# Softmax of the last attention block: half of its exponents taken head by head, with the maximum as bias and sums kept by ScalarE

## The chip, the cores and the metric

The kernel runs on one core of a Trainium2 chip. The core has five engines that run their own instruction queues in order and meet at semaphores: TensorE (PE, with weight loads shown as PEld), VectorE (DVE), ScalarE (ACT), GpSimd (POOL) and SyncE (SP, which issues the DMAs here). The metric is the device time of one execution in microseconds. The kernel before takes 341.5 us, the median of 3 runs that lie between 341.49 and 341.51.

## The reference

The inputs are `x` and `ctx_1024`, both 32 x 64 x 128, and a score bias of 32 x 16 x 64 x 64. Two layers follow each other. The first has two attentions with 16 heads of 8 columns and a feed-forward part, each followed by a layer norm; the second is one attention with 16 heads of 64 columns, the bias added twice:

```
def _L1_xattn_ref(q, k, v, bias, graph_attn_bias, wq, ...):     # both biases are the same array
    qh, kh, vh = heads of (q @ wq + bq), (k @ wk + bk), (v @ wv + bv)
    scores = einsum('bhqd,bhkd->bhqk', qh / sqrt(dk), kh) + bias + graph_attn_bias
    weights = softmax(scores, axis=-1)
    out = einsum('bhqk,bhkd->bhqd', weights, vh) @ wo + bo + q
    return layernorm(out) * ln_g + ln_b

x = _L0_xattn_ref(x, ctx_1024, ...)       # self attention, cross attention, feed-forward, 3 layer norms
x = _L1_xattn_ref(x, ctx_1024, ctx_1024, fside, fside, ...)
```

In the first layer a row is masked where it is all zero (`mask0`), which the kernel keeps as a sign per row.

## The kernel before, in words

The 32 sequences are taken in 16 pairs; one tile is a pair, 128 rows on 128 partitions. Each tile goes through three chains of steps, called A (self attention), B (cross attention and feed-forward) and C (the second layer). Each chain works on another tile at the same time: while C is at tile 5, A and B are some tiles ahead. Scores of a tile are 128 x 1024 numbers, 16 heads of 64; they are handled in two groups of 8 heads, called group 0 and group 1 below.

Group g of C's softmax goes through these steps. `fadd` (DVE, L973) adds bias and products in the tile `Sc`; `max` (DVE, L983) takes the maximum of each head into `C_mx`; `sub` (POOL, L1077) subtracts it from 128 x 512 scores in place; `exp` (ACT, L771) takes the exponent of 128 x 512 numbers with a scale of 2 into `Pc`; `den` (DVE, L991 and L993) sums each head into `C_den` and takes the reciprocal `C_rd`; `nrm` (POOL, L1086) multiplies. Then PE transposes the weights (`pt`, L609), ACT copies them from PSUM (`pts`, L780), PE multiplies them with the values (`zt`, L622), ACT copies (`zts`, L750), and PE makes the output projection (`o`, L632), which DVE adds to the residual (`y`, L1002). The last norm (L926 to L943 on DVE, L1033 to L1053 on POOL) and a store end the tile. From tile 12 on odd tiles of C use the score tile of A (`A_S`) and A's banks.

Chain A's `m0` step (DVE, L835 and L838) takes the largest magnitude of each row for four tiles at once and turns it into the sign, 128 x 4 numbers; it runs four times. PE has steps that only keep it at work: products of a zero tile, `K.warm` near the beginning (two products each) and `L.warm` at the end (three products each, `COOL` of them, L347), which wait for the last norm of chain B.

No scheduler runs on the chip: `PLAN` is a written list of about 1,900 words such as `C.exp_1#5`, chain, step and tile. Each engine walks through it and issues the steps that it has, so the list sets the order on all five queues. The steps wait for semaphores that count: `C.s_sub` goes up by one for each `sub`, `C.s_p` for each `exp`, `C.s_den` for each sum.

Of the kernel before, what the change touches and what calls it, by code (L numbers as in the profile page):

```python
# [1109 lines left out]
A.xh#0 A.gb#0 A.e#1 C.ks_1#3 C.clo#4 B.am#0 C.v_0#0 A.max_0#1 B.cm#0 A.qk#2 A.max_1#1 C.v_1#0 C.vs_0#0 A.q0#2  # L1110
A.sub_0#1 B.tr#0 A.e0#2 B.xts#0 A.sub_1#1 A.exp_0#1 B.qkv#0 A.nz#2 A.exp_1#1 A.cnt#2 A.pt_0#1 A.v#2 B.qk#0
A.pt_1#1 A.pts_0#1 B.q0#0 C.k_0#4 A.cut#2 A.pts_1#1 A.kblk#2 C.vs_1#0 A.pv_0#1 A.pv_1#1 B.e0#0 A.zts#1
C.ks_0#4 A.z#1 C.k_1#4 A.zn#1 C.k_0#5 A.y#1 C.ks_1#4 A.st#1 A.qkv#3 C.ks_0#5 B.nz#0 C.k_1#5 A.rstd#1 C.k_0#6
A.xh#1 C.ks_1#5 A.gb#1 B.cnt#0 A.e#2 B.cut#0 B.v#0 B.kblk#0 B.am#1 K.warm#5 A.qk#3 C.k_1#6 A.max_0#2 B.cm#1
C.ks_0#6 A.q0#3 B.tr#1 A.sub_0#2 A.e0#3 B.xts#1 A.max_1#2 C.ks_1#6 B.e#0 A.nz#3 A.exp_0#2 A.sub_1#2 A.cnt#3
B.qkv#1 B.max_0#0 A.exp_1#2 A.pt_0#2 B.max_1#0 B.qk#1 A.pt_1#2 A.pts_0#2 B.sub_0#0 C.k_0#7 A.pts_1#2 B.sub_1#0
B.exp_0#0 A.pv_0#2 A.pv_1#2 B.q0#1 A.v#3 B.e0#1 A.zts#2 A.cut#3 B.exp_1#0 A.z#2 B.pt_0#0 A.kblk#3 A.zn#2
B.pt_1#0 B.pts_0#0 B.nz#1 C.k_1#7 A.y#2 B.pts_1#0 A.st#2 B.cnt#1 C.ks_0#7 B.pv_0#0 B.cut#1 B.pv_1#0 A.rstd#2
C.v_0#1 B.v#1 B.zts#0 C.ks_1#7 B.kblk#1 A.xh#2 B.z#0 C.vs_0#1 A.e#3 B.zn#0 B.y#0 B.st#0 A.qkv#4 A.max_0#3
B.rstd#0 C.v_1#1 A.max_1#3 C.v_0#2 C.vs_1#1 B.xh#0 A.sub_0#3 A.qk#4 B.gb#0 B.e#1 C.vs_0#2 A.q0#4 A.sub_1#3  # L1120
A.exp_0#3 A.gb#2 B.f1#0 C.v_1#2 B.max_0#1 B.f1s#0 A.exp_1#3 B.max_1#1 B.f2#0 A.pt_0#3 B.f2s#0 B.sub_0#1
A.pt_1#3 C.vs_1#2 B.sub_1#1 B.f3#0 B.exp_0#1 C.v_0#3 B.y3#0 B.exp_1#1 B.pt_0#1 A.pts_0#3 B.3st#0 B.pt_1#1
A.pts_1#3 B.am#2 B.3rstd#0 A.e0#4 B.pts_0#1 A.pv_0#3 B.pts_1#1 A.nz#4 A.pv_1#3 B.3xh#0 B.pv_0#1 B.cm#2 A.m0#4
B.pv_1#1 B.3gb#0 A.zts#3 A.cnt#4 B.tr#2 B.zts#1 A.z#3 A.cut#4 C.v_1#3 B.xts#2 C.vs_0#3 A.zn#3 A.kblk#4 B.z#1
C.vs_1#3 B.qkv#2 A.y#3 B.zn#1 C.bvo#0 B.qk#2 A.st#3 B.q0#2 B.y#1 A.rstd#3 B.st#1 A.v#4 B.rstd#1 B.e0#2 A.xh#3
C.obias#0 A.gb#3 A.qkv#5 B.nz#2 B.xh#1 B.cnt#2 C.x3t#0 B.cut#2 A.e#4 B.gb#1 C.x3ts#0 B.v#2 B.kblk#2 B.am#3
B.f1#1 A.qk#5 C.q_0#0 A.max_0#4 B.f1s#1 A.max_1#4 B.f2#1 C.q_1#0 A.sub_0#4 B.f2s#1 C.x3c#0 C.qs_0#0 A.sub_1#4
B.f3#1 B.e#2 B.y3#1 A.exp_0#4 A.q0#5 B.3st#1 A.exp_1#4 A.e0#5 B.max_0#2 C.qs_1#0 B.3rstd#1 A.pt_0#4 B.max_1#2
A.pt_1#4 A.pts_0#4 B.sub_0#2 C.e#0 B.cm#3 B.3xh#1 B.exp_0#2 B.sub_1#2 B.3gb#1 A.pts_1#4 B.tr#3 C.fadd_0#0
# [174 lines left out]
```

## Times and the profile before

| | us |
|---|---|
| median of the runs | 341.5 |
| the profiled execution, its own time | 341.61 |
| its span, first to last instruction | 339.8 |
| granted TensorE clock, mean over the span | 0.995 of 2.4 GHz |
| PE busy | 320.3 (94%) |
| DVE busy | 291.3 (86%) |
| POOL busy | 241.6 (71%) |
| ACT busy | 239.9 (71%) |

The profile is of one execution. Its span leaves out 1.8 us of the execution's own time. Busy time is the union of an engine's instructions, so two that overlap count once; an instruction's duration can therefore be longer than the distance from its start to the next one's. In PE's case a matmul's latency is in its duration, so short waits between matmuls do not show as idle time.

### The profile page before, as it was taken

The page shows a single profiled execution, that of the slowest core. Times are in us where ns is not written, and L with a number is a line of the kernel's source. Part 1 is how long each engine was busy: PE and PEld are TensorE (multiplying, and loading weights), DVE is VectorE, ACT ScalarE, POOL GpSimd, SP SyncE. Part 2 cuts the span into 40 slices and gives each one's busy share as a digit, 9 for nine tenths or more (in the row PEclk, how much of TensorE's full clock was granted, in tenths as well). Part 3 has the DMA queues.
Part 4 walks back from the last instruction along what each step waited for, and adds up shares of the span by engine and source line. Part 5 has one row for each costly group of instructions (what it writes and reads, how often), then busy time and mean ns, then how long its engine had stood idle before and what let it go on. Part 6 is the DMA issues. An engine that isn't in the chain of part 4 may idle for free.

```text
span 339.8 us, 13231 instructions
## 1 busy us (share of the span) xinstructions
PE 320.3 (94%) x5328; PEld 252.3 (74%) x5333; DVE 291.3 (86%) x836; ACT 239.9 (71%) x567; POOL 241.6 (71%) x376
## 2 busy tenths in 40 slices
...
GB/s 154 332 327 210 3 0 2 3 65 4 2 4 133 2 4 2 88 57 12 54 4 3 2 141 4 11 3 33 103 2 5 0 143 3 3 17 136 2 2 31
DMA packets 13180, 17.87 MB, mean 53 GB/s; under 512 B 1601, under 2 KB 10177, under 8 KB 13121
## 3 DMA queue, kind: packets, MB, share of 16 engines
...
q14 instruction: 18, 0.14, 0.1%
...
## 4 chain that ended last, share of the span: by engine, by line
PE 56%; DVE 26%; ACT 5%; issue 5%; POOL 4%; DMA 1%; SPq 1%; POOLq 0%; ACTq 0%; DVEq 0%
PE C_E L632 5%; PE C_E L577 4%; PE B_E L451 3%; PE C_E L622 3%; PE A_E L432 3%; PE B_E L432 3%; PE C_E L593 2%; DVE A_mx L889 2%; PE A_E L451 2%; DVE A_S L897 2%; PE C_E L609 2%; PE B_E L465 2%; DVE Sc L973 2%; DVE C_den L991 2%; DVE L_xh L943 2%
## 5 line engine op out<-in xcount | busy, mean ns | idle before, releaser
L1025 POOL TENSOR_TENSOR A_kblk<-A_qk,cst 128x1024 f32<-128x1024 f32 x16 | 30.3, 1897 | 25.5 <-DVE A_qk L865 25.4
L1046 POOL TENSOR_TENSOR L_xg<-L_xh,vec_sb 128x128 f32<-128x128 f32 x64 | 29.2, 456 | 15.9 <-DVE L_xh L943 13.9
L1035 POOL TENSOR_TENSOR L_rstd<-L_ve,cst 128x1 f32<-128x1 f32 x64 | 35.1, 548 | 5.0
L1077 POOL TENSOR_TENSOR Sc<-Sc,C_mx 128x512 f32<-128x512 f32 x28 | 29.1, 1046 | 9.4 <-DVE C_mx L983 9.3
L763 ACT ACTIVATE qT<-C_E,bq 128x128 f32<-128x128 f32 x112 | 31.9, 379 | 4.1 <-PE C_E L577 3.9
L1033 POOL TENSOR_TENSOR L_ve<-L_mv,cst 128x1 f32<-128x1 f32 x64 | 12.1, 189 | 29.4 <-DVE L_mv L930 28.8
L1086 POOL TENSOR_TENSOR Pc<-Pc,C_rd 128x512 f32<-128x512 f32 x28 | 29.0, 1043 | 2.8 <-DVE C_rd L993 2.5
L1025 POOL TENSOR_TENSOR B_kblk<-B_qk,cst 128x1024 f32<-128x1024 f32 x16 | 30.3, 1897 | 0.0
L577 PE MATMUL C_E<-x3T,wq_sb 128*128 128x128 f32 x224 | 29.6, 279 | 0.4 <-ACT x3T L755 0.4
L577 PEld LDWEIGHTS C_E<-x3T,wq_sb 128*128 128x128 f32 x224 | 27.0, 192 | 1.1 <-ACT x3T L755 0.7
L632 PE MATMUL C_E<-wo_sb,C_zT 128*128 128x128 f32 x224 | 27.5, 276 | 0.1
L632 PEld LDWEIGHTS C_E<-wo_sb,C_zT 128*128 128x128 f32 x224 | 26.1, 192 | 0.7 <-ACT C_zT L750 0.6
L664 ACT ACTIVATE B_S<-B_S 128x512 f32<-128x512 f32 x32 | 19.8, 634 | 3.7 <-DVE B_S L897 3.5
L889 DVE TENSOR_REDUCE A_mx<-A_E 128x8 f32<-128x512 f32 x32 | 21.0, 680 | 1.6 <-PE A_E L439 1.5
L897 DVE TENSOR_TENSOR A_S<-A_E,A_mx 128x512 f32<-128x512 f32 x32 | 21.4, 683 | 0.3
L670 ACT COPY A_PT<-A_E 128x512 f32<-128x512 f32 x32 | 18.2, 592 | 4.1 <-PE A_E L451 3.7
L897 DVE TENSOR_TENSOR B_S<-B_E,B_mx 128x512 f32<-128x512 f32 x32 | 21.0, 679 | 0.0
L889 DVE TENSOR_REDUCE B_mx<-B_E 128x8 f32<-128x512 f32 x32 | 20.9, 679 | 0.0
L664 ACT ACTIVATE A_S<-A_S 128x512 f32<-128x512 f32 x32 | 20.1, 640 | 1.0 <-DVE A_S L897 1.0
L991 DVE TENSOR_REDUCE C_den<-Pc 128x8 f32<-128x512 f32 x28 | 18.7, 667 | 1.5 <-ACT Pc L771 1.5
L750 ACT COPY C_zT<-C_E 128x512 f32<-128x512 f32 x28 | 15.5, 590 | 6.1 <-PE C_E L622 5.9
L973 DVE TENSOR_TENSOR Sc<-f,C_E 128x512 f32<-128x512 f32 x28 | 18.4, 679 | 0.9 <-PE C_E L593 0.9
...
## 6 DMA issues: line engine op xcount, KB each, us to landing
...
```

The lines of the kernel that those rows point to most:

```text
L577: last = mm(place(n).E[g][:, j * P:(j + 1) * P], wq_sb[:, c:c + P], place(n).x3T[:], start=True, stop=True)
L632: last = mm(place(n).E[0][:, 0:D], place(n).zT[:, j].rearrange("p b c -> p (b c)"), wo_sb[:, j], start=(j == 0), stop=(j == J - 1))
L664: act.activation(v, v, ACT.Exp, scale=float(DK0) ** -0.5).then_inc(a.s_p, 1)
L763: last = act.activation(place(n).qT[:, 4 * g + j], place(n).E[g][:, j * P:(j + 1) * P], ACT.Identity, bias=bq8[:, 4 * g + j:4 * g + j + 1] ...
L889: dve.tensor_reduce(m, heads((a.E, a.X)[hf][:, :]), AX.X, ALU.max).then_inc(a.s_max, 1)
L897: tt(heads(a.S[:, hf * HALF:(hf + 1) * HALF]), heads((a.E, a.X)[hf][:, :]), m.unsqueeze(2).to_broadcast([P, 8, S]), ALU.subtract).then_inc ...
L991: dve.tensor_reduce(d, heads(place(n).P[:, g * HALF:(g + 1) * HALF]), AX.X, ALU.add).then_inc(C.s_den, 1)
L1025: tt(a.kblk[:], a.qk[:, 1].unsqueeze(1).to_broadcast([P, 8, P]), at["rmask"].unsqueeze(2).to_broadcast([P, 8, P]), ALU.mult).then_inc(a.s_ ...
L1035: tt(l.rstd[:], l.ve[:], at["power"], ALU.pow).then_inc(l.s_rstd, 1)
L1046: tt(l.xg[:], l.xh[:], l.g, ALU.mult).then_inc(l.s_xg, 1)
L1077: tt(v, v, place(n).mx[:, 8 * g:8 * g + 8].unsqueeze(2).to_broadcast([P, 8, S]), ALU.subtract).then_inc(C.s_sub, 1)
L1086: tt(pr, pr, place(n).rd[:, 8 * g:8 * g + 8].unsqueeze(2).to_broadcast([P, 8, S]), ALU.mult).then_inc(C.s_nrm, 1)
```

## The change

Group 0 is as before. For group 1 POOL no longer subtracts: it multiplies the 128 x 8 maxima by -2 (a new constant column, `twice`), and ACT takes the exponent in eight instructions of 128 x 64, one for each head, each with that head's column as bias and with the sum of its results written to `C_den`. DVE's sum of group 1 goes away, its reciprocal stays. The sign of `m0` is made by comparing with a tile of zeros in place of a comparison with a constant. There are nine `L.warm` steps in place of six. `PLAN` is a new list: the same steps and three more, in another order throughout.

```diff
-COOL = 6
+COOL = 9
-CONST = dict(ident=P, hmask=H, rmask=H // 2, bsel=2, trow=1, own=2, power=1, eps0=1, eps1=1)
+CONST = dict(ident=P, hmask=H, rmask=H // 2, bsel=2, trow=1, own=2, power=1, eps0=1, eps1=1, twice=1)
...
+        "twice": np.full((P, 1), -2.0),
...
             def c_exp(g):
                 def step(n):
-                    act.wait_ge(C.s_sub, 2 * n + 1 + g)
-                    act.activation(place(n).P[:, g * HALF:(g + 1) * HALF], place(n).S[:, g * HALF:(g + 1) * HALF],
-                                   ACT.Exp, scale=2.0).then_inc(C.s_p, 1)
+                    o = place(n)
+                    if g == 0:
+                        act.wait_ge(C.s_sub, 2 * n + 1)
+                        act.activation(o.P[:, 0:HALF], o.S[:, 0:HALF], ACT.Exp, scale=2.0).then_inc(C.s_p, 1)
+                    else:
+                        act.wait_ge(C.s_sub, 2 * n + 2)
+                        for h in range(8, 16):
+                            last = act.activation(o.P[:, h * S:(h + 1) * S], o.S[:, h * S:(h + 1) * S], ACT.Exp, scale=2.0,
+                                                  bias=o.mx[:, h:h + 1], accum_out=o.den[:, h:h + 1])
+                        last.then_inc(C.s_p, 1)
...
-                ts(m0s[:, n:n + FIRST], am0[:, n:n + FIRST], 0.0, None, ALU.is_gt).then_inc(s_m0, 1)
+                tt(m0s[:, n:n + FIRST], am0[:, n:n + FIRST], blank[:, 0:FIRST], ALU.is_gt).then_inc(s_m0, 1)
...
-                    dve.tensor_reduce(d, heads(place(n).P[:, g * HALF:(g + 1) * HALF]), AX.X, ALU.add).then_inc(C.s_den, 1)
-                    dve.wait_ge(C.s_den, 2 * n + 1 + g)
+                    if g == 0:
+                        dve.tensor_reduce(d, heads(place(n).P[:, 0:HALF]), AX.X, ALU.add).then_inc(C.s_den, 1)
+                        dve.wait_ge(C.s_den, n + 1)
                     dve.reciprocal(place(n).rd[:, 8 * g:8 * g + 8], d).then_inc(C.s_rd, 1)
...
                     pool.wait_ge(C.s_max, 2 * n + 1 + g)
+                    if g == 1:
+                        m = place(n).mx[:, 8:16]
+                        tt(m, m, at["twice"].to_broadcast([P, 8]), ALU.mult).then_inc(C.s_sub, 1)
+                        return
...
-K.warm#0 A.qkv#0 K.warm#1 A.qk#0 A.q0#0 A.e0#0 A.nz#0 A.cnt#0 C.whi#0 K.warm#2 A.cut#0 A.v#0 C.chi#0 K.warm#3
+A.qkv#0 A.qk#0 A.q0#0 A.e0#0 A.nz#0 A.cnt#0 K.warm#0 A.cut#0 C.chi#0 A.v#0 C.whi#0 K.warm#1 A.kblk#0 K.warm#2
...
```

In the built program each of the 128 new exponents is two instructions on ACT, the exponent and a read of its sum; the lists below show the pair as one. Line numbers of the changed kernel are some 1 to 13 higher.

The first place is ACT's queue at C's tile 5, before: both exponents of that tile (`Pc`), the queries of tile 6 (`qT`), keys (`kT0`), and the copies of the transposed weights (`PTc`).

```order
L691 COPY xc<-B_J 128x256
L771 ACTIVATE Pc<-Sc 128x512
L670 COPY B_PT<-B_E 128x512
L771 ACTIVATE Pc<-Sc 128x512
L657 COPY B_qk<-B_J 128x256
L763 ACTIVATE qT<-C_E,bq8 128x128 x4
L676 COPY B_zT<-B_E 128x256
L763 ACTIVATE qT<-C_E,bq8 128x128 x4
L731 ACTIVATE kT0<-A_E,bk_sb 128x512 x2
L780 COPY PTc<-C_E 128x512 x2
```

The same place of the changed kernel:

```order
L774 ACTIVATE Pc<-Sc 128x512
L665 ACTIVATE B_S<-B_S 128x512
L677 COPY A_zT<-A_E 128x256
L692 COPY xc<-B_J 128x256
L756 COPY x3T0<-C_E 128x128
L671 COPY B_PT<-B_E 128x512
L658 COPY B_qk<-B_J 128x256
L778 ACTIVATE Pc,C_den0<-Sc,C_mx0 128x64 x8
L677 COPY B_zT<-B_E 128x256
L764 ACTIVATE qT<-C_E,bq8 128x128 x8
L732 ACTIVATE kT0<-A_E,bk_sb 128x512 x2
L788 COPY PTc<-C_E 128x512 x2
```

Six instructions now stand between the two exponents where one stood; behind the eight small ones come the copy of B's result, all eight query instructions, the keys and the two copies that PE waits for.

The second place is DVE's queue at the same tile, before: the sums (`C_den0`) and reciprocals (`C_rd0`) of both groups among steps of A and B.

```order
L991 TENSOR_REDUCE C_den0<-Pc 128x8
L993 RECIPROCAL C_rd0<-C_den0 128x8
L852 TENSOR_SCALAR A_nz<-A_J 128x128
L943 TENSOR_SCALAR L1_xh<-A_E,L1_mv,L1_rstd 128x128
L844 TENSOR_TENSOR B_q0<-cst,B_J 128x32
L991 TENSOR_REDUCE C_den0<-Pc 128x8
L993 RECIPROCAL C_rd0<-C_den0 128x8
```

And in the changed kernel:

```order
L1000 TENSOR_REDUCE C_den0<-Pc 128x8
L1002 RECIPROCAL C_rd0<-C_den0 128x8
L915 RECIPROCAL A_rd<-A_E 128x16
L919 SCALAR_TENSOR_TENSOR A_E<-A_E,m0s,A_rd 128x128
L927 TENSOR_TENSOR A_E<-A_E,xs 128x128
L852 TENSOR_TENSOR B_q0<-cst,B_J 128x32
L934 BN_STATS L1_st<-A_E 128x6
L938 BN_AGGR L1_mv<-L1_st 128x2
L884 TENSOR_TENSOR A_V0<-A_J,cst 128x32
L887 TENSOR_TENSOR A_V0<-A_J,A_V0 128x32x8
L951 TENSOR_SCALAR L1_xh<-A_E,L1_mv,L1_rstd 128x128
L1002 RECIPROCAL C_rd0<-C_den0 128x8
```

The second sum is gone, and nine instructions stand between the two reciprocals where three and the sum stood.

The third place is the end of PE's queue, before: `Pc` and `PTc` belong to tile 14, `A_S`, `A_PT` and `wk_sb` to tile 15.

```order
L609 MATMUL C_E<-cst,Pc 128x128 x4
L593 MATMUL A_E<-kT1,A_kblk 64x64 x32
L609 MATMUL C_E<-cst,Pc 128x128 x4
L347 MATMUL B_E<-blank 128x512 x3
L622 MATMUL C_E<-PTc,C_V2 64x64 x32
L347 MATMUL B_E<-blank 128x512 x6
L632 MATMUL C_E<-wo_sb,C_zT 128x128 x8
L609 MATMUL A_E<-cst,A_S 128x128 x8
L622 MATMUL A_E<-A_PT,C_V3 64x64 x32
L632 MATMUL A_E<-wo_sb,wk_sb 128x128 x8
```

And in the changed kernel:

```order
L610 MATMUL C_E<-cst,Pc 128x128 x4
L610 MATMUL A_E<-cst,A_S 128x128 x4
L348 MATMUL B_E<-blank 128x512 x3
L610 MATMUL A_E<-cst,A_S 128x128 x4
L348 MATMUL B_E<-blank 128x512 x3
L623 MATMUL C_E<-PTc,C_V2 64x64 x32
L623 MATMUL A_E<-A_PT,C_V3 64x64 x32
L348 MATMUL B_E<-blank 128x512 x3
L633 MATMUL C_E<-wo_sb,C_zT 128x128 x8
L633 MATMUL A_E<-wo_sb,wk_sb 128x128 x8
```

Tile 14's products with the values and its output projection have moved behind tile 15's transposes, with three idle products after these and three more after the products with the values.

## Rows read from the trace of the kernel before

**Rows 1.** Busy time by stage: start:end, length, then PE, PEld, DVE, ACT, POOL busy (instructions), clock, DMA.

```profile
50.00:300.00 250.00, 245.34 (x4325) 199.58 (x4322) 233.17 (x682) 188.79 (x463) 193.30 (x302) 1.00 0.09 30
300.00:339.80 39.80, 30.19 (x575) 24.46 (x577) 22.59 (x59) 19.89 (x48) 27.70 (x50) 0.96 0.13 40
```

**Rows 2.** The page's chain of work that ended last, shares by engine.

```profile
PE 56%; DVE 26%; ACT 5%; issue 5%; POOL 4%; DMA 1%; SPq 1%; POOLq 0%; ACTq 0%; DVEq 0%
```

**Rows 3.** That chain within 62 to 122 us, shares by line.

```profile
by line: issue 13.4%; DVE A_mx L889 8.2%; DVE A_S L897 8.1%; DVE Sc L973 7.5%; DVE L_xh L943 5.9%; DVE L_st L926 5.0%; DVE C_den L991 4.9%; DVE C_mx L983 4.6%; DVE B_mx L889 4.3%; DVE B_S L897 4.3%; DVE B_V L879 2.2%; DVE L_mv L930 2.1%; DV
```

**Rows 4.** DVE in order of time (start, us, what): y of C's tiles 1 and 10.

```profile
105.37 0.29 DVE L1002 TENSOR_TENSOR L_y<-C_E,x3r 128x128 f32<-128x128 f32 x1
...
277.81 0.29 DVE L1002 TENSOR_TENSOR L_y<-C_E,x3r 128x128 f32<-128x128 f32 x1
```

**Rows 5.** DVE in order of time: sum and reciprocal of group 1, C's tile 0.

```profile
74.97 0.63 DVE L991 TENSOR_REDUCE C_den<-Pc 128x8 f32<-128x512 f32 x1
75.64 0.20 DVE L993 RECIPROCAL C_rd<-C_den 128x8 f32<-128x8 f32 x1
75.75 0.38 DVE L943 TENSOR_SCALAR L_xh<-A_E,L_mv,L_rstd 128x128 f32<-128x128 f32 x1
```

**Rows 6.** DVE groups: line, what, count | busy us, mean ns | idle before.

```profile
L991 DVE TENSOR_REDUCE C_den<-Pc 128x8 f32<-128x512 f32 x28 | 18.7, 667 | 1.5 <-ACT Pc L771 1.5
```

**Rows 7.** POOL groups.

```profile
L1046 POOL TENSOR_TENSOR L_xg<-L_xh,vec_sb 128x128 f32<-128x128 f32 x64 | 29.2, 456 | 15.9 <-DVE L_xh L943 13.9 <-DVE L_xh L940 1.6
L1077 POOL TENSOR_TENSOR Sc<-Sc,C_mx 128x512 f32<-128x512 f32 x28 | 29.1, 1046 | 9.4 <-DVE C_mx L983 9.3
...
L1033 POOL TENSOR_TENSOR L_ve<-L_mv,cst 128x1 f32<-128x1 f32 x64 | 12.1, 189 | 29.4 <-DVE L_mv L930 28.8
```

**Rows 8.** ACT groups.

```profile
L763 ACT ACTIVATE qT<-C_E,bq 128x128 f32<-128x128 f32 x112 | 31.9, 379 | 4.1 <-PE C_E L577 3.9
...
L670 ACT COPY A_PT<-A_E 128x512 f32<-128x512 f32 x32 | 18.2, 592 | 4.1 <-PE A_E L451 3.7
...
L771 ACT ACTIVATE Pc<-Sc 128x512 f32<-128x512 f32 x28 | 17.7, 634 | 2.0 <-POOL Sc L1077 1.9
...
L676 ACT COPY A_zT<-A_E 128x256 f32<-128x256 f32 x16 | 6.0, 375 | 4.4 <-PE A_E L465 4.4
...
L755 ACT COPY x3T<-C_E 128x128 f32<-128x128 f32 x14 | 3.7, 265 | 6.3 <-PE C_E L564 6.3
```

**Rows 9.** ACT in order of time, 71 to 94 us; xN are merged, us from first to last.

```profile
72.75 1.16 ACT L771 ACTIVATE Pc<-Sc 128x512 f32<-128x512 f32 x2
...
90.10 0.27 ACT L755 COPY x3T<-C_E 128x128 f32<-128x128 f32 x1 [0.40 <-PE C_E L564]
90.27 0.63 ACT L771 ACTIVATE Pc<-Sc 128x512 f32<-128x512 f32 x1
...
91.81 2.15 ACT L763 ACTIVATE qT<-C_E,bq 128x128 f32<-128x128 f32 x8
```

**Rows 10.** The sign step's line: duration in ns min/median/max.

```profile
L838 DVE TENSOR_SCALAR m0s<-am x4: 170/646/1027, 18.5 to 173.9; 128x4 f32<-128x4 f32 x4
```

**Rows 11.** The chain in order of time at the end: start, us, what.

```profile
319.86 1.04 ACT A_kblk L763 x4
...
322.74 0.59 PE B_E L347 x2
...
325.18 0.54 ACT A_S L771
...
325.74 0.70 DVE C_den L991
...
326.75 2.06 POOL A_S L1086 x2
...
330.19 1.21 PE A_E L622 x64
...
332.54 2.06 PE A_E L632 x16
```

More of the change, by code:

```diff
@@ L1110 @@
[L1110 to L1129, printed above, removed]
@@ new lines @@
+B.cm#1 A.q0#3 A.max_1#2 B.tr#1 A.e0#3 A.sub_0#2 B.xts#1 B.e#0 A.sub_1#2 A.exp_0#2 A.nz#3 A.exp_1#2 A.cnt#3
+B.qkv#1 B.max_0#0 C.ks_1#6 A.pt_0#2 B.max_1#0 B.qk#1 A.pt_1#2 A.pts_0#2 B.sub_0#0 C.k_0#7 A.pts_1#2 B.q0#1
+B.sub_1#0 B.exp_0#0 A.pv_0#2 A.pv_1#2 A.cut#3 B.e0#1 A.zts#2 B.exp_1#0 A.kblk#3 A.z#2 B.pt_0#0 A.zn#2 B.pt_1#0
+B.pts_0#0 C.k_1#7 A.y#2 B.nz#1 B.pts_1#0 A.st#2 B.cnt#1 C.ks_0#7 B.pv_0#0 B.cut#1 A.rstd#2 B.pv_1#0 C.v_0#1
+A.v#3 B.zts#0 B.kblk#1 C.ks_1#7 A.xh#2 B.z#0 B.v#1 C.vs_0#1 A.e#3 B.zn#0 B.y#0 A.qkv#4 B.st#0 C.v_1#1
@@ new lines @@
+A.max_0#3 B.rstd#0 A.qk#4 A.q0#4 C.v_0#2 A.max_1#3 C.vs_1#1 A.gb#2 B.xh#0 A.e0#4 A.sub_0#3 B.gb#0 B.e#1
+A.sub_1#3 A.exp_0#3 B.am#2 C.vs_0#2 B.f1#0 C.v_1#2 B.max_0#1 A.exp_1#3 B.f1s#0 B.sub_0#1 A.pt_0#3 C.vs_1#2
+B.f2#0 B.max_1#1 C.v_0#3 B.exp_0#1 A.nz#4 B.f2s#0 B.sub_1#1 A.pt_1#3 B.cm#2 A.pts_0#3 B.f3#0 B.pt_0#1 B.y3#0
+B.exp_1#1 C.v_1#3 A.pts_1#3 B.3st#0 B.pt_1#1 B.pts_0#1 B.3rstd#0 A.cnt#4 A.pv_0#3 B.pts_1#1 A.cut#4 A.pv_1#3
+B.pv_0#1 C.vs_0#3 B.3xh#0 B.pv_1#1 A.v#4 A.zts#3 B.tr#2 B.3gb#0 B.zts#1 A.z#3 B.xts#2 B.z#1 C.vs_1#3 A.zn#3
@@ new lines @@
+B.qkv#2 A.kblk#4 B.zn#1 C.bvo#0 B.qk#2 A.y#3 B.q0#2 A.st#3 B.y#1 A.rstd#3 B.st#1 B.e0#2 C.obias#0 B.rstd#1
+A.xh#3 A.qkv#5 B.nz#2 B.xh#1 B.cnt#2 C.x3t#0 B.cut#2 A.e#4 C.x3ts#0 B.gb#1 B.v#2 A.gb#3 B.f1#1 A.qk#5
+A.max_0#4 C.q_0#0 B.f1s#1 A.q0#5 B.kblk#2 A.sub_0#4 B.f2#1 C.q_1#0 A.max_1#4 B.f2s#1 A.exp_0#4 B.am#3 B.f3#1
+C.qs_0#0 A.sub_1#4 A.e0#5 B.y3#1 B.e#2 A.exp_1#4 A.nz#5 B.3st#1 C.qs_1#0 A.pt_0#4 B.max_0#2 B.3rstd#1 A.pt_1#4
+B.max_1#2 A.pts_0#4 C.e#0 C.x3c#0 B.cm#3 B.3xh#1 A.pts_1#4 B.sub_0#2 B.3gb#1 B.tr#3 C.fadd_0#0 B.exp_0#2
@@ new lines @@
+A.pv_0#4 A.pv_1#4 B.sub_1#2 B.xts#3 A.cnt#5 B.pt_0#2 A.zts#4 C.max_0#0 B.exp_1#2 A.z#4 B.qkv#3 A.cut#5
+B.pts_0#2 C.sub_0#0 B.pt_1#2 A.zn#4 B.qk#3 B.pv_0#2 B.pts_1#2 B.q0#3 A.kblk#5 C.fadd_1#0 C.exp_0#0 B.pv_1#2
+A.y#4 C.loadf#0 C.max_1#0 C.x3t#1 B.e0#3 C.x3ts#1 B.zts#2 A.st#4 B.z#2 B.nz#3 C.sub_1#0 A.rstd#4 C.den_0#0
+C.exp_1#0 B.cnt#3 C.q_0#1 B.zn#2 C.nrm_0#0 C.q_1#1 A.xh#4 B.y#2 C.qs_0#1 C.den_1#0 B.st#2 A.e#5 C.nrm_1#0
+A.v#5 C.qs_1#1 B.cut#3 B.rstd#2 A.qkv#6 A.max_0#5 B.kblk#3 C.pt_0#0 A.qk#6 B.xh#2 B.v#3 C.pt_1#0 C.pts_0#0
@@ new lines @@
+A.st#6 B.e0#5 B.y#4 A.rstd#6 C.qs_0#3 B.st#4 C.q_1#3 C.den_1#2 B.nz#5 B.rstd#4 A.xh#6 B.cnt#5 A.e#7 C.qs_1#3
+C.nrm_1#2 B.xh#4 B.v#5 B.cut#5 B.gb#4 C.pt_0#2 C.pt_1#2 A.max_0#7 C.pts_0#2 C.x3c#2 B.f1#4 C.v_0#5 A.qk#8
+B.kblk#5 B.f1s#4 A.q0#8 C.pts_1#2 A.sub_0#7 B.f2#4 C.v_1#5 C.st#1 B.f2s#4 C.vs_0#5 A.max_1#7 B.f3#4 C.vs_1#5
+C.zt#2 A.gb#6 B.y3#4 A.exp_0#7 A.sub_1#7 B.e#5 C.rstd#1 C.zts_0#2 B.am#6 C.zts_1#2 B.3st#4 A.e0#8 B.max_0#5
+B.cm#6 B.3rstd#4 A.exp_1#7 C.e#3 A.nz#8 B.sub_0#5 B.3xh#4 B.exp_0#5 A.pt_0#7 C.fadd_0#3 B.3gb#4 B.tr#6
@@ new lines @@
+C.o#3 B.sub_0#6 B.3xh#5 B.exp_0#6 B.sub_1#6 B.3gb#5 A.zn#8 B.exp_1#6 B.tr#7 B.pt_0#6 A.y#8 B.xts#7 B.pt_1#6
+A.st#8 B.pts_0#6 B.qkv#7 C.y#3 A.rstd#8 B.pts_1#6 C.max_1#4 C.x3t#5 B.pv_0#6 C.x3ts#5 A.nz#9 B.pv_1#6 B.qk#7
+C.sub_1#4 A.xh#8 A.cnt#9 C.q_0#5 B.zts#6 A.cut#9 A.gb#8 C.exp_1#4 C.den_0#4 C.k_0#9 A.kblk#9 C.st#3 B.z#6
+C.k_1#9 A.v#9 C.ks_0#9 C.q_1#5 B.zn#6 C.qs_0#5 C.nrm_0#4 C.den_1#4 B.q0#7 B.y#6 A.qkv#10 B.st#6 C.ks_1#9
+B.e0#7 C.qs_1#5 B.rstd#6 A.e#9 B.nz#7 C.nrm_1#4 B.xh#6 B.cnt#7 C.pt_0#4 A.qk#10 A.max_0#9 C.gb#2 C.pt_1#4
@@ new lines @@
+C.den_0#7 B.qk#10 B.exp_1#9 A.y#11 C.q_1#8 B.pts_0#9 C.nrm_0#7 A.st#11 C.qs_0#8 C.den_1#7 B.q0#10 B.pt_1#9
+A.v#12 A.rstd#11 B.e0#10 B.pts_1#9 C.nrm_1#7 A.xh#11 B.pv_0#9 C.qs_1#8 B.pv_1#9 B.nz#10 B.cnt#10 C.k_0#12
+A.gb#11 B.v#10 B.zts#9 A.cut#12 C.pt_0#7 C.ks_0#12 B.z#9 C.pt_1#7 A.kblk#12 C.pts_0#7 B.zn#9 A.qkv#13
+C.pts_1#7 C.k_1#12 B.y#9 B.st#9 B.cut#10 C.zt#7 C.ks_1#12 C.x3c#7 B.am#11 B.rstd#9 C.st#6 A.e#12 C.zts_0#7
+B.xh#9 C.zts_1#7 B.gb#9 C.e#8 A.qk#13 A.max_0#12 C.gb#5 A.sub_0#12 B.f1#9 C.v_0#10 A.max_1#12 B.f1s#9
@@ new lines @@
+B.e0#11 B.pts_1#10 C.y#7 A.y#12 B.pv_0#10 C.exp_1#8 B.nz#11 B.pv_1#10 A.st#12 B.cnt#11 C.q_0#9 C.st#7
+A.rstd#12 C.den_0#8 C.q_1#9 B.zts#10 C.x3c#8 C.qs_0#9 C.den_1#8 A.xh#12 C.nrm_0#8 A.v#13 B.z#10 C.k_0#13
+C.qs_1#9 B.zn#10 C.nrm_1#8 C.k_1#13 B.y#10 B.v#11 C.ks_0#13 A.qkv#14 A.gb#12 B.st#10 C.pt_0#8 C.ks_1#13
+B.cut#11 C.pt_1#8 B.rstd#10 C.pts_0#8 B.am#12 A.e#13 C.pts_1#8 B.xh#10 B.gb#10 C.zt#8 A.qk#14 A.max_0#13
+A.max_1#13 B.kblk#11 B.f1#10 C.v_0#11 A.q0#14 A.sub_0#13 B.f1s#10 C.zts_0#8 B.f2#10 A.sub_1#13 C.v_1#11
@@ new lines @@
+A.qk#15 C.gb#7 C.zt#9 A.exp_0#14 A.q0#15 B.max_0#12 A.exp_1#14 A.gb#13 B.max_1#12 B.f2s#11 A.pt_0#14 C.zts_0#9
+B.sub_0#12 B.f3#11 C.zts_1#9 A.pt_1#14 B.y3#11 B.exp_0#12 A.e0#15 B.3st#11 A.pts_0#14 C.e#10 B.sub_1#12
+A.pts_1#14 B.3rstd#11 A.nz#15 B.exp_1#12 B.am#13 B.pt_0#12 B.3xh#11 B.cm#13 A.cnt#15 B.pt_1#12 C.fadd_0#10
+B.pts_0#12 B.3gb#11 B.tr#13 C.fadd_1#10 B.pts_1#12 A.pv_0#14 B.pv_0#12 B.xts#13 C.max_0#10 A.pv_1#14
+C.loadf#10 B.pv_1#12 A.zts#14 A.cut#15 C.x3t#11 C.sub_0#10 B.zts#12 B.qkv#13 C.max_1#10 A.z#14 B.qk#13 B.z#12
```

247 lines of the change are left out of this document (111 added, 136 removed).

## The prediction

> **What bounds the kernel now.** I read the busy time by stage first, then the chain of waits, then single queues in order of time. Between 50 and 300 us all three chains run, and there PE is busy 245.3 of 250 us, DVE 233.2, POOL 193.3 and ACT 188.8 [rows 1]: 98%, 93.3%, 77% and 75.5%. PE's figure contains matmul latency, so it hides short waits; DVE's does not, and DVE is as good as full. The chain of waits agrees: PE has 56% of it and DVE 26%, ACT and POOL only 5% and 4% [rows 2], and in one stretch of 60 us it runs along DVE almost without a break, with no other engine among its eleven costliest lines [rows 3]. So there are two limits that alternate, PE and DVE, and two engines with room. One tile of C passes every 19.16 us: its `y` step starts at 105.37 us for tile 1 and at 277.81 us for tile 10, nine tiles later [rows 4]. Per tile that is 17.87 us of DVE (233.17/250 x 19.16) and 14.47 us of ACT (188.79/250 x 19.16).
>
> **The change part by part.** The sum is made against the profiled execution's own 341.61 us, 0.1 above the median of 341.5, a difference I neglect.
>
> *DVE.* One sum of 128x512 per tile goes. It holds the queue from 74.97 to 75.64 us, when the reciprocal behind it starts [rows 5]: 0.67 us, and its mean duration is 0.667 us [rows 6]. The reciprocal stays. Over 16 tiles that is 10.7 us of DVE, and per tile DVE falls from 17.87 to 17.20 us. What this is worth depends on how much of the time DVE sets the pace. The lower end counts only the chain's DVE share: 26% of 339.8 us is 88 us, 4.6 tiles, so 3.1 us. The upper end lets DVE set the pace of all 13 tiles whose softmax runs before 300 us, at the density it reaches now: 13 x 0.67/0.933 = 9.3 us. The two ends have equal claim, since the stretch of rows 3 speaks for the upper and PE's 56% for the lower; I take the middle, 6.2 us.
>
> *POOL.* A subtraction of 1.046 us becomes a product of 128x8. Between 189 ns for one column and 456 ns for 128 [rows 7] eight columns come to 0.20 us, so POOL loses 0.84 us per tile. POOL is 4% of the chain, and I count nothing for it in the middle; it lets group 1's exponents start earlier, which I use for the end.
>
> *ACT.* The exponent of 128x512 takes 0.634 us [rows 8]; two in a row take 1.16 us [rows 9], so one holds the queue 0.53 us. Nearest to the new form are the query instructions: 128x128, with a bias read from a tile. Eight of them take 2.15 us [rows 9], each 0.379 us long [rows 8], so they start (2.15 - 0.379)/7 = 0.253 us apart. A column costs (592 - 375)/256 = 0.85 ns [rows 8], 64 columns fewer save 0.054 us: 0.199 us per exponent. The read of the sum is in no row. Its lower bound is nothing, its upper bound a whole 128x128 copy with no overlap, 0.265 us. That copy lets the next instruction start 0.17 us after it [rows 9], of which 0.11 us are its columns, so a small instruction holds the queue some 0.06 us; near this I take 0.10. A pair is then 0.30, eight are 2.4 us, and ACT gains 1.87 us per tile, 30 us in all; its load goes from 14.47 to 16.34 us of 19.16, 85%. The bounds of a pair are 0.2 and 0.59 us (0.379 - 0.054 alone, then 0.265). The cover is ACT's idle time, 4.7 us per tile: where it holds, the price is nothing. What stands behind the eight pairs is a copy for B, all queries, the keys and the copies of the transposed weights, for which PE waits. Where ACT is on the chain already, 5% or 17 us, its load grows by 13%, which is 2.2 us; I take that end, because the queue is in order and nothing overtakes the eight pairs.
>
> The Trainium skill's page "ScalarE: Activation LUTs", section "What ACT_TABLE_LOAD costs", gives an instruction with such a bias 280 ns and 0.833 ns per column, with an overlap of 93 ns. The query rows are near it in length, 379 against 387 ns, but start 253 and not 294 ns apart; by the page a pair would be an estimated 0.34 us, the group 2.7, and the sum 0.4 us higher.
>
> *Sign step.* Its four instructions last from 170 to 1027 ns, median 646 [rows 10], for 128x4 numbers, so something holds up three of them. If the new form is never held, DVE saves at most some 0.5 us four times, of which those within a DVE stretch count; if it is held as before, nothing. I take nothing.
>
> On what holds it the Trainium skill's page "SBUF — State Buffer", section "Who interferes with whom", has a rule that speaks against the edit: a comparison with a constant can use the port pair that DVE shares with GpSimd, but an instruction with two inputs in SBUF waits for GpSimd's reads as well, and both tiles here lie in SBUF. The spread of rows 10 fits the first half; no row shows the second.
>
> *New order.* It has no row. In the middle it can gain at most PE's idle time, 250 - 245.3 = 4.7 us, and I allow it the same as a loss; value nothing.
>
> *End.* From 326.75 us the chain runs through two normalisations of tile 15 on POOL, its products with the values and its projection [rows 11]. Until then old and new come out even. Tile 14's second exponent can follow the queries at 320.9 us less the 0.5 us of the exponent that stood between them, and ends by 322.8. Tile 15's first one starts at 325.18 in the old order, behind a copy (such a copy takes 0.59 us [rows 8]) that the new order puts later; without it, it ends at 325.1, the eight pairs end at 327.5, the sum of 0.70 is gone, and after the reciprocal and the second half of POOL's 2.06 us tile 15's weights are ready at 327.5 + 0.2 + 1.03 = 328.7, against 328.8. But in the new order PE has tile 14's products with the values, its projection and idle products still ahead of tile 15's. Two idle products took 0.59 us on the chain already, products with the values 1.21, a projection 2.06 [rows 11]. About 0.6 us of this delays tile 15's products (the rest lies beside the copy they wait for) and 0.8 us its projection (tile 14's runs while tile 15's result is copied): 1.4 us, an estimate. At worst, with three idle products and a full projection in line, it is about 4; at best nothing.
>
> *Sum.* 341.6 - 6.2 + 2.2 + 1.4 = 339.0 us.
>
> **The rivals.**
>
> *DVE sets the pace throughout.* Then 9.3 us come off, ACT's additions stay within its idle time, and the end costs 1.4: 333.7 us. For it: DVE's 93.3% in 250 us and the unbroken stretch of rows 3. Against it: PE's 56% of the chain.
>
> *PE sets the pace.* Whatever leaves DVE turns into idle time of DVE, and gains and losses cancel: 3.1 us off, 2.2 for ACT, 1.4 at the end, 342.1, or with 0.6 us from the new order 341.5. For it: PE's 98%. Against it: that figure hides waits, and the chain leaves PE for 44% of the time.
>
> *ACT becomes the bound (slower).* Place: the eight pairs in ACT's queue. If the read waits until its exponent has left the engine, the two do not overlap. ACT's load per tile is 14.47 - 0.53 + 8 pairs; it reaches the 17.87 us that DVE has now when a pair takes 0.49 us, and from there on the kernel is slower. At 0.52 ACT has 18.10 us per tile, at DVE's density 19.40 us instead of 19.16: 13 x 0.24 = 3.1 us, and at the end 1.4 + 8 x 0.22 = 3.2, with no gain from DVE: 347.9 us. At the bound of 0.59 it is 18.66, 20.0 per tile, 11 us and 3.7 at the end: about 356. For it: an unknown instruction eight times a tile, and everything behind it in an in-order queue. Against it: ACT's instructions do overlap (379 ns long, 253 apart). Below 0.49 it still eats up the gain step by step.
>
> A rule of the skill goes this way: the page "VectorE: DVE Perf Modes", section on the TRN2 errata, says that ScalarE and VectorE pay a fixed latency for each instruction with a source in SBUF, and advises tiles of 512 elements or more, the size that is cut into eight here. The rows of copies agree with a fixed part, 265 ns for 128 columns and 592 for 512.
>
> **How the numbers follow.** The forecast, part of DVE's relief comes out, has a chance of 0.43, with 336 to 340.8 us as its own range. DVE throughout has 0.14, PE as the bound 0.15, ACT as the bound 0.28. A measurement of this kernel can tell about 0.2%, 0.7 us, from no change. The first two cases lie below 340.8, so faster has 0.57; the third is no change, 0.15; the fourth slower, 0.28. The range for 8 in 10 runs from 333.5, just under the second case, to 346, within the fourth, which leaves out the heavier half of that one and the far end of the upper bound for DVE.
>
> **What would show it.** The new exponents should stand in the ACT groups with eight starts of 0.3 us, 2.4 us per tile with their reads; ACT at some 84% between 50 and 300 us and DVE still above 91%, with tiles 18.6 to 18.9 us apart. POOL's groups should have 16 products of about 0.2 us and 16 subtractions left. If pairs take 0.5 us or more, if ACT's share of the chain goes well beyond 10%, or DVE's density falls below 90%, the forecast is wrong towards slower; if tiles are 18.5 us apart or less, the second case was right. If tile 15's projection starts much over 2 us behind its normalisation's place in the old trace, I have sized the end too low.

## The result, and the profile after

The changed kernel takes 355.5 us (354.6 to 355.9), against 341.5 before: a ratio of 1.040, with a 95% interval from 1.036 to 1.043. It is slower by 14 us, where 2.5 us less had been forecast, and outside the range of 333.5 to 346.

The first thing to read is again the busy time by stage of the changed kernel (start:end, length, then PE, PEld, DVE, ACT, POOL busy), which answers to [rows 1]:

```profile
50.00:300.00 250.00, 240.34 (x4199) 192.86 (x4199) 219.01 (x646) 206.41 (x630) 175.31 (x292) 1.00 0.10 31
```

DVE has fallen from 233 to 219 us of 250, POOL from 193 to 175, and ACT has risen from 189 to 206. DVE is at 88% now and ACT at 83%; PE has lost 5 us of busy time in the same stretch and is at 96%. Two signs that the prediction had named against itself are there: DVE under 90%, and below, ACT's share of the chain over 10%. The changed kernel's chain of waits, by engine and by its costliest lines, answers to [rows 2]:

```profile
PE 56%; ACT 18%; DVE 13%; issue 6%; POOL 5%; DMA 1%; SPq 1%; POOLq 0%; DVEq 0%
ACT Pc L778 8%; PE A_E L433 4%; PE C_E L623 4%; PE C_E L633 3%; PE B_E L433 3%; PE C_E L610 3%; PE C_E L594 3%; PE A_E L452 3%; PE B_E L452 3%; PE B_E L348 2%; PE A_E L466 2%; PE B_E L466 2%; PE C_E L578 2%; ACT qT L764 2%; DVE A_S L905 1%
```

PE kept its share, DVE gave up half of its 26%, and ACT took what DVE gave up: it went from 5% to 18%, of which the new line alone has 8%. In order of time the chain goes through the eight exponents and their reads as one piece of some 2.65 us, in nine of the tiles between 50 and 300 us. Two of these pieces (start, us, what):

```profile
111.19 2.66 ACT Pc L778 x16
...
248.49 2.67 ACT Pc L778 x16
```

ACT's queue in order of time at the first of them shows what a pair is (start, us, what):

```profile
111.08 0.35 ACT L778 ACTIVATE Pc<-Sc,C_mx 128x64 f32<-128x64 f32 x1
111.33 0.19 ACT L778 ACTIVATION_READ_ACCUMULATOR Pc<-Sc,C_mx 128x1 f32 x1
111.42 0.34 ACT L778 ACTIVATE Pc<-Sc,C_mx 128x64 f32<-128x64 f32 x1
...
113.74 0.60 ACT L764 ACTIVATE qT<-C_E,bq 128x128 f32<-128x128 f32 x2
```

A read starts 0.24 us after its exponent, and the next exponent 0.09 us after the read, so a pair holds the queue 0.33 us, and the group from 111.08 to 113.74, 2.66 us. The groups of the changed kernel (count | busy us, mean ns | idle before) that answer to [rows 6 to 8]:

```profile
L778 ACT ACTIVATE Pc<-Sc,C_mx 128x64 f32<-128x64 f32 x112 | 37.3, 337 | 2.4 <-POOL C_mx L1087 2.4
...
L778 ACT ACTIVATION_READ_ACCUMULATOR Pc<-Sc,C_mx 128x1 f32 x112 | 21.2, 189 | 0.0
...
L1000 DVE TENSOR_REDUCE C_den<-Pc 128x8 f32<-128x512 f32 x14 | 9.4, 670 | 0.6 <-ACT Pc L774 0.6
L1002 DVE RECIPROCAL C_rd<-C_den 128x8 f32<-128x8 f32 x32 | 6.4, 199 | 7.2 <-ACT Pc L778 3.9 <-ACT A_S L778 2.6
...
L1087 POOL TENSOR_TENSOR C_mx<-C_mx,cst 128x8 f32<-128x8 f32 x16 | 3.4, 211 | 4.1 <-DVE C_mx L991 4.1
```

The removed work is gone as forecast, half of DVE's sums and half of POOL's subtractions, and POOL's new product takes 211 ns. Where the time goes can be read from C's `y` step. Its tiles 1 and 10 in the changed kernel's DVE queue, to be set beside [rows 4]:

```profile
110.20 0.28 DVE L1011 TENSOR_TENSOR L_y<-C_E,x3r 128x128 f32<-128x128 f32 x1
...
285.28 0.28 DVE L1011 TENSOR_TENSOR L_y<-C_E,x3r 128x128 f32<-128x128 f32 x1
```

Tile 1 is 4.8 us late already, tile 10 is 7.5 us late (19.45 us per tile, not 19.16), and the span ends 13.7 us late. So the loss comes in every stage: 4.8 us before tile 1's `y`, 2.6 in the nine tiles after it, 6.2 from there on.

### The profile page after: what moved, and what is told of

It is laid out like the page before. It is cut to its first block, busy times and chain, and to the rows that moved or that the text cites. A ratio compares the mean times of both kernels' runs of the same rounds, so it can differ in the third digit from the quotient of the medians.

```text
span 353.5 us, 13472 instructions
## 1 busy us (share of the span) xinstructions
PE 327.8 (93%) x5336; PEld 255.1 (72%) x5342; DVE 281.9 (80%) x820; ACT 269.7 (76%) x807; POOL 227.9 (64%) x376
## 4 chain that ended last, share of the span: by engine, by line
PE 56%; ACT 18%; DVE 13%; issue 6%; POOL 5%; DMA 1%; SPq 1%; POOLq 0%; DVEq 0%
ACT Pc L778 8%; PE A_E L433 4%; PE C_E L623 4%; PE C_E L633 3%; PE B_E L433 3%; PE C_E L610 3%; PE C_E L594 3%; PE A_E L452 3%; PE B_E L452 3%; PE B_E L348 2%; PE A_E L466 2%; PE B_E L466 2%; PE C_E L578 2%; ACT qT L764 2%; DVE A_S L905 1%
## 5 line engine op out<-in xcount | busy, mean ns | idle before, releaser
L778 ACT ACTIVATE Pc<-Sc,C_mx 128x64 f32<-128x64 f32 x112 | 37.3, 337 | 2.4 <-POOL C_mx L1087 2.4
L764 ACT ACTIVATE qT<-C_E,bq 128x128 f32<-128x128 f32 x112 | 30.8, 372 | 1.6 <-PE C_E L578 1.6
L1090 POOL TENSOR_TENSOR Sc<-Sc,C_mx 128x512 f32<-128x512 f32 x14 | 14.6, 1046 | 10.7 <-DVE C_mx L991 10.7
L778 ACT ACTIVATION_READ_ACCUMULATOR Pc<-Sc,C_mx 128x1 f32 x112 | 21.2, 189 | 0.0
L433 PE MATMUL A_E<-A_kblk,A_qk 64*64 64x512 f32 x128 | 17.8, 624 | 2.1 <-ACT kT L732 1.4
```

Of the source, the lines that this page charges most:

```text
L433: last = mm(bank[S * b:S * b + S, :], a.qk[r, 0, S * b:S * b + S], a.kblk[r, :, S * b:S * b + S], start=True, stop=not causal, skip_group_ ...
L764: last = act.activation(place(n).qT[:, 4 * g + j], place(n).E[g][:, j * P:(j + 1) * P], ACT.Identity, bias=bq8[:, 4 * g + j:4 * g + j + 1] ...
L778: last = act.activation(o.P[:, h * S:(h + 1) * S], o.S[:, h * S:(h + 1) * S], ACT.Exp, scale=2.0, bias=o.mx[:, h:h + 1], accum_out=o.den[: ...
```

## The experiments

Besides the forecast's mechanisms two theories were on the table. Theory 1: the eight exponents and their reads on ACT are the loss. Theory 2: the new order is the loss, whatever instructions stand in it. The first four runs cross the two: two orders, each with the old instructions, the new ones, and with a form that relieves DVE and POOL and holds ACT hardly longer.

**The old instructions in the new order.** The kernel before with the new list:

```diff
-PLAN = (list of the kernel before)
+PLAN = (list of the changed kernel)
-COOL = 6
+COOL = 9
```

> The old instructions in the new order (with nine idle steps at the end). Theory 1 (the eight exponents and their sum reads on ACT are the loss): without them the new order costs little, 340 to 345 us. Theory 2 (the new order is the loss, whatever stands in it): 350 us or more, near the 355.5 of the changed kernel.

354.9 us, ratio 1.038 (1.035 to 1.042). As theory 2 said: the new list costs 13 us with the old instructions in it. The chain of this run has PE at 45%, DVE at 31%, POOL at 13% and ACT at 1%, so with the old instructions the new list loses along DVE and POOL and not along ACT.

**The new instructions in the old order.** The changed kernel with the list of the kernel before.

> The new instructions in the old order. Theory 1: as slow as the changed kernel or slower, 353 to 362 us, since the old order was written for a short exponent. Theory 2: near the kernel before, 339 to 346 us.

370.0 us, ratio 1.082 (1.075 to 1.089): slower than theory 1 expected, and far from theory 2. The new instructions cost 28 us in the old list.

**One exponent in the old order.**

```diff
-                        for h in range(8, 16):
-                            last = act.activation(o.P[:, h * S:(h + 1) * S], ..., bias=o.mx[:, h:h + 1], accum_out=o.den[:, h:h + 1])
+                        last = act.activation(o.P[:, HALF:2 * HALF], o.S[:, HALF:2 * HALF], ACT.Exp, scale=2.0, bias=o.mx[:, 8:9])
...
-                    dve.reciprocal(place(n).rd[:, 8 * g:8 * g + 8], d)
+                    dve.reciprocal(place(n).rd[:, 8 * g:8 * g + 8], place(n).den[:, 0:8])
```

> Old order; group 1's exponent is one instruction of 128x512 with one bias column, and DVE takes the reciprocals of group 0's sums for it: the maxima of the heads and the sums of group 1 are left out. So DVE and POOL have their relief and ACT pays 0.1 us and not 2.2 us per tile. Theory 1 as forecast (DVE's relief is worth 6 us where nothing else grows): 334 to 338 us. Rival (PE sets the pace and the relief is worth nothing): 340 to 342 us.

341.07 us against 341.79, ratio 0.9978 (0.9964 to 0.9992). The relief of DVE and POOL, almost free of cost, is worth 0.7 us here; the forecast's lower end was 3.1. Busy time by stage and chain of this run, to be read against [rows 1, 2]:

```profile
50.00:300.00 250.00, 245.67 (x4329) 200.03 (x4326) 225.69 (x671) 190.29 (x465) 183.30 (x303) 1.00 0.09 30
```

```profile
PE 62%; DVE 20%; ACT 6%; POOL 5%; issue 4%; DMA 1%; SPq 1%; POOLq 0%; ACTq 0%; DVEq 0%
```

DVE's busy time falls by 7.5 us in the stretch, PE's stays, and PE's share of the chain rises by what DVE's falls: the freed time became idle time of DVE. That is the rival in which PE sets the pace, in this order.

**One exponent in the new order.** The same edit of the changed kernel.

> The same instructions as in the run with one exponent in the old order, here in the new order; the same parts are left out. Theory 1: the loss is gone, 333 to 342 us. Theory 2: 348 us or more, the order alone keeps the loss.

345.2 us, ratio 1.011 (1.006 to 1.015), between the two theories. Its four executions lie between 343.7 and 346.5, so differences to this run are good to some 1.5 us. Three steps then add up to the result. The relief in the old order: 341.8 to 341.1. The new order with the relief: 341.1 to 345.2, 4.1 us more. The eight pairs in the new order: 345.2 to 355.5, 10.3 us. And in the new order the relief is worth 9.7 us (354.9 to 345.2), in the old one 0.7: what an instruction costs depends on the list that was written around it. In the old list the pairs cost 28.9 us (341.1 to 370.0). The three steps are therefore one way of several to divide the loss: with the new instructions in both lists the new list is 14.5 us the better one (370.0 to 355.5). The chain of the run with one exponent in the new order shows the reverse of the changed kernel's, ACT at 2%:

```profile
PE 67%; DVE 16%; POOL 7%; issue 5%; ACT 2%; DMA 1%; SPq 1%; POOLq 0%; DVEq 0%
```

Where the new list costs its 4.1 us can be read from `y` of tiles 1 and 10 in this run, to be set beside [rows 4]:

```profile
107.83 0.28 DVE L1009 TENSOR_TENSOR L_y<-C_E,x3r 128x128 f32<-128x128 f32 x1
...
277.48 0.28 DVE L1009 TENSOR_TENSOR L_y<-C_E,x3r 128x128 f32<-128x128 f32 x1
```

That is 18.85 us per tile, less than the 19.16 before and within the 18.6 to 18.9 that had been forecast. The old list with one exponent has these steps at 105.32 and 276.96 and its end at 339.1 us: in the traces the new list loses 2.5 us before tile 1's `y`, gains 2.0 in the next nine tiles and loses 2.3 behind tile 10's, up to its end at 341.9 us (this trace is of the fastest of the four executions). Measured against it the pairs cost 2.4, 5.4 and 3.8 us in these three stretches.

What about the pairs costs? They hold ACT's queue, and they make group 1's result later. The next runs part the two.

**Exponents without reads, old order.**

```diff
-                                                  bias=o.mx[:, h:h + 1], accum_out=o.den[:, h:h + 1])
+                                                  bias=o.mx[:, h:h + 1])
```

> Old order, eight exponents with their bias but without the sums, so without the eight reads; DVE takes the reciprocals of group 0's sums (group 1's sums are left out). ACT is held about 2.0 us per tile (8 starts some 0.24 us apart), between the 0.64 us of one exponent and 2.7 us of eight pairs. If time follows ACT's hold in proportion: 341.1 + 28.9 x (2.0 - 0.64)/(2.7 - 0.64) = 360 us. If the reads alone are the loss: 341 to 345 us.

353.7 us, ratio 1.035 (1.032 to 1.038). Eight exponents without reads take 2.02 us in this run's trace, so they start 0.24 us apart, and hold the queue 1.9 us. The reads are not the loss alone: 12.7 us come with the exponents, 16.2 more with the reads, which add only 0.75 us per tile.

**A hold behind one exponent, old order.**

```diff
                         last.then_inc(C.s_p, 1)
+                        for h in range(n % 2 * 6, n % 2 * 6 + 6):
+                            act.activation(spare[h][:], iota[:], ACT.Exp, scale=-1.0, bias=at["eps0"], accum_out=sums[:, h:h + 1])
```

> Old order, one exponent for group 1 as in the run with one exponent (maxima by head and group 1's sums left out), and directly behind it, after its signal, six pairs of exponent and read on a tile that nobody waits for: ACT is held 2.6 us, but group 1's result is there after 0.7 us. If what costs is that everything behind in ACT's queue waits: 362 to 370 us, near the 370 of the new instructions in this order. If what costs is group 1's own later result: 341 to 345 us.

365.7 us, ratio 1.071 (1.066 to 1.075): 24.6 of the 28.9 us return although group 1's result is there early. The chain of this run has ACT at 24%. What the queue behind the hold stops shows in PE's waits between 50 and 300 us (PE's line, the ACT instruction waited for: us in total, times, longest). Waits that a matmul's latency hides are not in such a list. The first line is the only one for ACT in the run with one exponent in this order, the others are the four longest with the new instructions in this order:

```profile
PE C_E L623 <- ACT PTc L786: 0.9, 3, 0.5
...
PE B_E L466 <- ACT B_PT L671: 4.3, 3, 1.9
PE B_E L477 <- ACT B_zT L677: 3.8, 5, 1.5
PE C_E L610 <- ACT qT L764: 2.6, 3, 1.7
PE A_E L433 <- ACT kT L732: 2.0, 1, 2.0
```

With the new instructions PE's listed waits for ACT add up to 14.6 us, with the hold behind one exponent to 14.9, for the same copies of B, queries and keys. DVE, on the other hand, sits idle for 17.7 us in front of its reciprocals with the new instructions and for only 1.9 us here. So in this order most of the loss is there without the late result.

**The same in the new order.**

> The same instructions in the new order. If the queue behind is what costs: 352 to 356 us, near the changed kernel. If it is group 1's own result: near the 345.2 us of one exponent in this order.

352.6 us, ratio 1.031 (1.029 to 1.034): 7.4 of the 10.3 us. The queue behind the pairs is the larger part in both orders. PE's listed waits for ACT between 50 and 300 us are 6.3 us here, 5.0 in the changed kernel and 1.2 with one exponent in this order. The rest fits group 1's later result, which no run delays alone: DVE is idle in front of its reciprocals for 7.2 us in the changed kernel and for 0.6 in the other two.

**The sign step alone.**

```diff
-                ts(m0s[:, n:n + FIRST], am0[:, n:n + FIRST], 0.0, None, ALU.is_gt)
+                tt(m0s[:, n:n + FIRST], am0[:, n:n + FIRST], blank[:, 0:FIRST], ALU.is_gt)
```

> The kernel before with the new sign step alone. Forecast: nothing, within 0.7 us of 341.5. If the comparison with a tile is never held up: 339.5 to 341 us.

341.79 us against 341.87, ratio 0.999 (0.997 to 1.001), no change. Its line in that run, durations in ns min/median/max, to be set beside [rows 10]:

```profile
L838 DVE TENSOR_TENSOR m0s<-am,blank x4: 161/644/1021, 18.8 to 174.2; 128x4 f32<-128x4 f32 x4
```

The comparison of two tiles is held as long as the comparison with a constant was. In both traces the three held ones end 0.02 to 0.03 us after a POOL product of 1.90 us (`kblk`) that was running when they started; at the short one, no `kblk` was running.

**The changed kernel with six idle steps.**

```diff
-COOL = 9
+COOL = 6
```

> The changed kernel with six idle steps in place of nine, so the three between and behind the last transposes are gone. In its trace idle products stand on the chain of waits after 337 us with 1.28 + 1.13 + 0.59 us. If these delay the end: 352.5 to 354.5 us. If they only fill waits: 355 to 356 us.

355.6 us, ratio 1.039 (1.036 to 1.043), as the changed kernel. The idle products stand on the changed kernel's chain, at 337.86, 340.19 and 343.50 us, but only fill waits. The chain goes back to the instruction before on the same engine when no release ended a wait just then, so work that merely stood in front of a waiting instruction is counted there too.

**The kernel before with three idle steps.** The same constant, 6 to 3.

> The kernel before with three idle steps in place of six (one that stands on its chain of waits with 0.59 us is gone). If idle products lie on the way to the end: 340.3 to 341.2 us. If they hold up the clock at the end: 342 us or more.

341.9 us against 341.7, ratio 1.0005 (0.998 to 1.003): no change, so neither.

**The hold spread out, old order.** One pair each behind six ACT steps of a tile:

```diff
+            for k, name in enumerate(("A.exp_1", "A.zts", "B.exp_1", "B.zts", "C.exp_1", "C.zts_1")):
+                steps[name] = and_pair(steps[name], k)
```

> Old order, one exponent for group 1 (maxima by head and group 1's sums left out), and the same six pairs per tile on a tile that nobody waits for, but one pair each behind six different steps of ACT (both second exponents of A and B, their result copies, C's second exponent and its second result copy). If ACT's total load is what costs: as in the run with the six pairs together, 362 to 368 us. If the unbroken hold at that one place costs: 343 to 352 us.

349.5 us, ratio 1.022 (1.018 to 1.025). With the same added work on ACT 8.4 us are lost, not 24.6: in the old order 16 us are due to where, and how close together, the pairs stand. PE's listed waits for ACT are 5.3 us in this run, not 14.9.

**The hold together, at a later place, old order.**

```diff
+            steps["C.qs_1"] = and_pairs(steps["C.qs_1"])
```

> Old order, one exponent for group 1 (maxima by head and group 1's sums left out), and the same six pairs together, unbroken, on a tile that nobody waits for; but they stand behind the second four query instructions of the next tile, so behind both groups of queries and the copy of B's result that stood behind the hold before. If what costs is that queries and the copy of B's result wait: 345 to 353 us. If any unbroken hold of 2 us costs the same: 363 to 368 us.

361.6 us, ratio 1.060 (1.058 to 1.062). Only 4 us come back, so it does not hang on the queries and B's copy behind the pairs; an unbroken hold of 2 us costs 25 us at one place of this list and 21 at the other. PE now waits for what stands behind the new place, 12.9 us in all between 50 and 300 us, the keys and the transposed weights above all:

```profile
PE A_E L434 <- ACT kT L733: 3.4, 2, 2.0
PE C_E L624 <- ACT PTc L787: 2.9, 6, 0.9
```

**The changed kernel with its pairs in two groups of four.** Each ACT step is followed by up to four of the pairs that are left:

```diff
+            def split(name, step):
+                def both(n):
+                    if name in ("C.exp_0", "C.exp_1"):
+                        some(8)
+                    step(n)
+                    some(4)
+                return both
```

> The changed kernel complete, but with the eight pairs in two groups of four, one ACT step of the list between them (for most tiles the first four queries of the next tile, a copy for B, or keys): no hold is longer than 1.35 us, group 1's result comes 0.5 to 1 us later, ACT's total is the same. If the length of an unbroken hold is what costs: 349 to 353 us. If group 1's later result or ACT's total load is what costs: 355 to 358 us.

361.5 us, ratio 1.055 (1.051 to 1.059): slower than the 355.5 of the unbroken group by 5 to 6 us, and beyond both expectations. In the new order breaking the hold does not help. What grew is DVE's idle time in front of its reciprocals, from 7.2 us in the changed kernel to 15.1:

```profile
L1019 DVE RECIPROCAL C_rd<-C_den 128x8 f32<-128x8 f32 x32 | 6.4, 200 | 15.1 <-ACT Pc L775 10.3 <-ACT A_S L775 4.3
```

So group 1's result, later by one ACT step, is the likely cost, argued from this wait and not shown apart.

**The hold spread out, new order.**

> New order, one exponent for group 1 (maxima by head and group 1's sums left out), six pairs on a tile that nobody waits for, one each behind six different ACT steps of a tile. If the unbroken hold costs: 346 to 350 us, clearly under the 352.6 us of the six pairs together. If the new order has made room for the pairs at their own place only: 353 us or more.

351.4 us, ratio 1.027 (1.022 to 1.033), against 352.6 and 1.031 (1.029 to 1.034) for the hold together: between the two expectations, and no difference that these runs can tell. The old order's answer does not carry over. There spreading brought 16 us; here the added work costs 6 us spread and 7 together. Why, these runs do not show.

No run that does the whole work beats the kernel before. The relief alone, with group 1's maxima and sums left out, is worth 0.7 us in the old order, and every form that pays for it on ACT costs more.

## Why the prediction was wrong, point by point

*DVE as a limit, 6.2 us.* Wrong, and with it the reading of [rows 1, 3]. DVE was 93% busy and the chain ran along it for 60 us, but with DVE and POOL relieved almost for nothing only 0.7 us came off in the order of that time. (In the new order the same relief is worth 9.7 us, so this term cannot be priced apart from the list; DVE's part and POOL's were not measured apart.) A share of the chain says who ended a wait in that execution; it does not say that the next in line is far behind. PE was next at once: its share went from 56% to 62%. The lower bound of 3.1 us, made from the chain's share, was no bound. What came true in this order is the rival in which PE sets the pace.

*ACT's group, 2.4 us.* It measured 2.66. The pair is 0.33 and not 0.30 us, since a read holds the queue 0.09 us and an exponent 0.24. By the Trainium skill's page "ScalarE: Activation LUTs", section "What ACT_TABLE_LOAD costs", such an exponent is an estimated 333 ns long, with 240 ns between starts; measured are 337 ns and 0.24 us, so the page came closer than my 0.20 us from the query rows. Those rows, and the copies that the slower rival shows for a fixed part, read what PE wrote to PSUM; the exponents read SBUF tiles. From 337 ns for 64 columns and 729 ns for 512, both with a bias column, an estimated 0.875 ns per column and 281 ns fixed follow for them.

*ACT's price, 2.2 us.* This is the step that failed most. It was made from ACT's share of the chain before, 5%, with ACT's idle time of 4.7 us per tile as cover for the rest. Measured, the pairs cost 10.3 us in the new order and 28.9 in the old one, with ACT at 83% and 78% busy between 50 and 300 us. The slower rival named the right place, the eight pairs in ACT's queue, but set its point at ACT being as full as DVE, 0.49 us for a pair; the loss came at 0.33. ACT's idle time was no cover, because the new work stands in one piece in front of copies, queries and keys that PE waits for: PE's listed waits for ACT rise from 0.9 to 14.6 us in the old order and from 1.2 to 5.0 in the new one. The runs with a hold on a tile that nobody waits for show the queue as the larger part: 24.6 of 28.9 us and 7.4 of 10.3.

*New order, nothing.* Wrong: 4.1 us with the relief in it, 13 us with the old instructions. Its bound, PE's 4.7 us of idle time either way, was exceeded in the second case. The traces place the loss before tile 1's `y` and behind tile 10's, with a gain of 2.0 us between them. What in the list costs it there is not shown; the crossed runs show only that each list fits its own instructions.

*POOL, nothing; sign step, nothing.* POOL's product took 211 ns (0.20 forecast). The sign step is no change, and the Trainium skill's page "SBUF — State Buffer", section "Who interferes with whom", agrees in so far as the form with two inputs in SBUF is held as long, and the held ones end with a GpSimd product, `kblk`, both of whose inputs lie in SBUF. Whether its reads hold them or something else of that product, no run here shows.

*End, 1.4 us.* From `y` of tile 13 to the end of the span the kernel before took 23.2 us (316.58 to 339.8) and the changed one 26.75 (326.75 to 353.5), 3.5 us more. The three idle steps have no part in it; with one exponent in the new order this stretch is 25.0 us, so about half comes with the order and half with the pairs.

The sum that the runs give, in this sequence of steps: 341.8 - 0.7 (relief) + 4.1 (order) + 10.3 (pairs) = 355.5 us; the end's 3.5 us are part of the last two. Against the forecast's 339.0 that is 8.1 us in ACT's price, 5.5 in DVE's relief and 4.1 in the order, less the end's 1.4, which stands in the others here, and with 0.2 of difference in the kernel before.
